# Graph attention and a mixture of experts on one core: one-hots moved from VectorE to ScalarE, segment ends kept on VectorE, weights turned one batch behind the scores

## The chip, the core and the metric

The kernel runs on one core of a Trainium2 chip. PE is TensorE, DVE is VectorE, ACT is ScalarE, POOL is GpSimd and SP is SyncE; SBUF is the working memory and PSUM the memory into which PE writes, here eight banks of 128 partitions x 512 fp32. The metric is the device time of one execution in microseconds (us), the median of three runs.

## The reference, cut to what matters

N = 2500 nodes, E = 80000 edges sorted by destination, H = 4 heads of 64 features.

```python
h = jnp.einsum('nf,hfo->nho', x, W)
e_s = jnp.einsum('nho,ho->nh', h, a_src); e_d = jnp.einsum('nho,ho->nh', h, a_dst)
scores = jax.nn.leaky_relu(e_s[edge_src] + e_d[edge_dst], 0.2)
m = jax.ops.segment_max(scores, edge_dst, num_segments=N)
ex = jnp.exp(scores - m[edge_dst])
denom = jax.ops.segment_sum(ex, edge_dst, num_segments=N)
msg = (ex / denom[edge_dst])[:, :, None] * h[edge_src]
agg = jax.ops.segment_sum(msg, edge_dst, num_segments=N)
x = x + relu(agg)                      # x was normalised before
...
x = x + moe(layernorm(x))              # 8 experts, the best 2 of each node
```

## The kernel before, in words

The execution has three stages. In the first, up to about 110 us, nodes are normalised and projected, a table `h_tab` of 260 fp32 a node (256 features and the 4 source scores) is written to memory, and the layout of the edges in tiles is computed. The third, from about 1142 us on, is the mixture of experts. The change is in the second stage, the edges.

**Edges.** There are 664 tiles (NT) of 128 edges, one edge a partition, laid out so that two neighbouring tiles belong to one block of 128 destination nodes. Eight tiles (BT) are a batch, four batches (PB) or 32 tiles (PH) a round, which the code calls a phase; there are 83 batches (NBAT) and 21 rounds (NPH), the last of 24 tiles.

**Fetches.** POOL fetches tile t with an indirect DMA (L503): for each of the 128 edges the row of `h_tab` of its source goes to slot t % 128 of `ring` in SBUF. It reads the row numbers from `srcP` in SBUF. From tile AHEAD = 80 on it waits, every eight tiles, until batch (t - AHEAD) / 8 is done (`batch_done`).

**Scores and weights of a round.** When all tiles of round f are there, ACT copies their source scores to `Ex` (L839); PE turns these and spreads the destination scores over the partitions (`scores_T`, L606, L610), into bank 6 (`soft`). The layout is now one row for each of 4 heads x 32 tiles. A segment's maximum is found with running maxima: DVE scans each row forwards and backwards (`scores`, L1091 to L1094), PE takes the rows' last columns to one partition (L614, L615), DVE scans along the tiles there (`chain`, L1101 to L1116), PE takes the carries back (`carries_T`, L620), and DVE scans again with them and forms the exponents (`weights`, L1120 to L1132). ACT takes the Exp (L845) and PE turns the weights back (`weights_T`, L631) into bank 5 or 7 (`exT`). If a segment crosses from one round to the next, what its block has collected is rescaled (`rescale`, L1138 to L1142).

**A batch.** DVE multiplies the fetched features in place with the weights and makes the one-hots of the destinations (`weigh`, L1151 to L1153); PE adds, for each pair of tiles, one-hot transposed times features into one of banks 0 to 3 (`batch`, L640); DVE adds the four banks into `acc` (`flush`, L1080). Bank 4 holds the numbers 0 to 127 for the comparison (`iota_ps`). `weigh` of a batch and `flush` of the one before alternate in an order written out by hand; every engine's queue runs in order, so the order of the calls in the loops of DVE, PE and ACT sets the order of the work.

```python
v.tensor_tensor(msg, msg, ex.unsqueeze(3).broadcast_to([P, BT, H, FO]), ALU.mult)
```

is the product of L1151: `msg` is `ring` in SBUF, and `ex` a part of `exT` in PSUM.

## Time and profile before

| | |
|---|---|
| median of 3 runs | 1513.36 us (1510.36 to 1515.03) |
| the profiled execution | 1508.79 us, its span 1507.0 us |
| mean granted clock of PE | 0.755 of full speed |
| busy: PE, DVE, ACT, POOL | 788.1, 757.1, 120.4, 792.2 us |
| fetches of tiles (L503) | 664, from 109.48 to 1067.2 us |
| last addition into `acc` | ends at 1141.8 us |

Busy times are of the whole span. Times in the rows are microseconds from the span's start. A row of the timeline has the start, the duration, the engine, line and operation, what it writes and reads with the shape, how many instructions are merged in the row, and in brackets how long the engine had stood idle before it and what released it. "issue" is time in which the engine waited for nothing that the profile shows, "remote" a release by something the profile can't name. The ends of matmuls are modelled.

### The profile page before, as it was taken

The page shows a single profiled execution, that of the slowest core. Times are in us where ns is not written, and L with a number is a line of the kernel's source. Part 1 is how long each engine was busy: PE and PEld are TensorE (multiplying, and loading weights), DVE is VectorE, ACT ScalarE, POOL GpSimd, SP SyncE. Part 2 cuts the span into 40 slices and gives each one's busy share as a digit, 9 for nine tenths or more (in the row PEclk, how much of TensorE's full clock was granted, in tenths as well). Part 3 has the DMA queues.
Part 4 walks back from the last instruction along what each step waited for, and adds up shares of the span by engine and source line. Part 5 has one row for each costly group of instructions (what it writes and reads, how often), then busy time and mean ns, then how long its engine had stood idle before and what let it go on. Part 6 is the DMA issues. An engine that isn't in the chain of part 4 may idle for free.

```text
span 1507.0 us, 10576 instructions
## 1 busy us (share of the span) xinstructions
PE 788.1 (52%) x2990; PEld 617.4 (41%) x2990; DVE 757.1 (50%) x1578; ACT 120.4 (8%) x289; POOL 792.2 (53%) x843
## 2 busy tenths in 40 slices
PE   0610204454654555644555644545567288888881
PEld 0500203333443343433433433334447266766661
DVE  5510206555576555676555765555878822222215
ACT  3400000000000000000000000000002221111110
POOL 6357763666666666766666766666200034434431
PEclk9865556767787767877768777778776589999985
DMA  8254332333333333333333333333270111111116
GB/s 305 84 74 115 108 85 57 93 91 97 103 95 92 93 97 91 103 94 90 94 97 93 101 94 91 94 98 99 85 265 12 64 44 56 53 52 54 54 48 218
DMA packets 76401, 144.34 MB, mean 96 GB/s; under 512 B 19951, under 2 KB 46749, under 8 KB 76221
## 3 DMA queue, kind: packets, MB, share of 16 engines
q0 software_dynamic: 39856, 110.32, 26.1%
q1 hardware_dynamic: 33909, 30.82, 6.9%
q10 hardware_dynamic: 2584, 2.56, 0.5%
q8 instruction: 25, 0.41, 0.1%
q14 instruction: 27, 0.22, 0.0%
HBM read 126.85 MB, written 17.43 MB: 96 GB/s over the span
## 4 chain that ended last, share of the span: by engine, by line
DVE 33%; another core or an unknown queue 22%; issue 18%; PE 12%; DMA 6%; POOL 5%; DVEq 3%; ACT 2%; SPq 0%; POOLq 0%
DVE acc L1080 8%; DVE shared L1153 6%; DMA ring<-z_tab,ring 4%; DVE ring L1151 4%; PE psum L640 3%; PE psum L736 3%; POOL ys_tab L523 3%; PE psum L750 2%; POOL ring L514 1%; DVEq L1080 1%; PE psum L724 1%; PE psum L569 1%; DVE shared L1387 1%; DVE ring L1152 1%
## 5 line engine op out<-in xcount | busy, mean ns | idle before, releaser
L503 POOL DMA_INDIRECT ring<-h_tab,srcP x664 | 629.1, 947 | 328.9 <-issue 190.1
L640 PE MATMUL psum<-ring,shared 128*128 128x260 f32 x1328 | 417.7, 483 | 236.4 <-DVE acc L1080 156.3
L640 PEld LDWEIGHTS psum<-ring,shared 128*128 128x128 f32 x1328 | 320.2, 247 | 325.1 <-DVE shared L1153 175.2
L1151 DVE TENSOR_TENSOR ring<-ring,psum 128x2048 f32<-128x2048 f32 x83 | 189.5, 2283 | 9.1 <-PE psum L631 2.4
L1080 DVE TENSOR_TENSOR acc<-acc,psum 128x260 f32 x332 | 140.1, 422 | 95.4 <-remote 44.1
L1091 DVE TENSOR_TENSOR_SCAN edY<-RS_all,psum 128x128 f32<-128x128 f32 x21 | 8.8, 421 | 300.8 <-remote 268.5
L523 POOL DMA_INDIRECT ys_tab<-shared,ring x54 | 56.2, 1040 | 150.2 <-DVE shared L1387 142.0
L514 POOL DMA_INDIRECT ring<-z_tab,ring x54 | 52.6, 973 | 151.3 <-DVEq L1367 135.2
L736 PE MATMUL psum<-ring 128*128 128x256 f32 x432 | 114.1, 423 | 29.4 <-DVE ring L1379 29.4
L614 PE MATMUL psum<-ident,Fw 128*1 128x128 f32 x21 | 7.8, 373 | 216.6 <-DVEq L1096 215.0
L1379 DVE TENSOR_SCALAR ring<-psum,tail_consts 128x256 f32<-128x256 f32 x54 | 26.9, 539 | 185.8 <-PE psum L724 182.6
L736 PEld LDWEIGHTS psum<-ring 128*128 128x128 f32 x432 | 89.5, 212 | 49.8 <-DVE ring L1379 36.0
L1153 DVE TENSOR_TENSOR shared<-psum,Dcol 128x1024 f32<-128x1024 f32 x83 | 100.6, 1212 | 0.0
L750 PE MATMUL psum<-ring,RS_all 128*128 x432 | 97.5, 379 | 0.0
L614 PEld LDWEIGHTS psum<-ident,Fw 128*1 128x1 f32 x21 | 1.7, 79 | 225.4 <-DVEq L1096 223.4
L750 PEld LDWEIGHTS psum<-ring,RS_all 128*128 128x128 f32 x432 | 82.1, 190 | 11.2
L888 ACT ACTIVATE RS_all<-psum,tail_consts 128x256 f32<-128x256 f32 x108 | 45.3, 470 | 209.0 <-PE psum L736 191.1
L843 ACT ACTIVATE fm<-old 1x4 f32<-1x4 f32 x20 | 4.1, 204 | 662.0 <-DVE old L1116 534.2
L610 PE MATMUL psum<-X,spread 32*128 32x128 f32 x168 | 43.7, 412 | 0.0
L610 PEld LDWEIGHTS psum<-X,spread 32*128 32x128 f32 x168 | 32.4, 208 | 8.3 <-issue 5.7
L485 POOL DMA_INDIRECT ed_tab<-e_node,spos x20 | 19.6, 982 | 30.6 <-DVE spos L1031 21.9
L724 PE MATMUL psum<-ident,ring 128*128 128x128 f32 x108 | 17.7, 288 | 21.0 <-DMA ring<-z_tab,ring 21.0
(290 smaller groups left out, 656.2 us busy)
## 6 DMA issues: line engine op xcount, KB each, us to landing
ring<-h_tab,srcP POOLq DMA_INDIRECT x664
ring<-in_L_ffn_W SPq DMA_DIRECT2D x16, 512.0 KB, 9.7
h_tab<-ring SPq DMA_DIRECT2D x10, 260.0 KB
ring<-in_x SPq DMA_DIRECT2D x1, 2432.0 KB
z_tab<-ring SPq DMA_DIRECT2D x2, 1024.0 KB, 4.4
ring<-ys_tab SPq DMA_DIRECT2D x4, 512.0 KB, 8.8
ring<-ys_tab ACTq DMA_DIRECT2D x4, 512.0 KB, 9.7
out<-acc SPq DMA_DIRECT2D x4, 512.0 KB
```

Source lines behind the costliest of these rows:

```text
L503: pool.indirect_dma_start(out=ring[:, t % RING, :], out_offset=None, in_=h_tab, in_offset=bass.IndirectOffsetOnAxis(ap=srcP[:, t:t + 1], a ...
L514: pool.indirect_dma_start(out=xs_in[:, u, m, :], out_offset=None, in_=z_tab, in_offset=bass.IndirectOffsetOnAxis(ap=node_ix[:, BM * j + m: ...
L523: pool.indirect_dma_start(out=ys_tab, out_offset=bass.IndirectOffsetOnAxis(ap=dest_ix[:, BM * j + m:BM * j + m + 1], axis=0), in_=y_out[:, ...
L610: last = pe.matmul(soft[:, P:2 * P], spread[:, first:first + P], seeds[:, h, :], start=(h == 0), stop=(h == H - 1))
L640: last = pe.matmul(bank[g][:, 0:MW], dst_oh[:, n % OHB, 2 * g + r, :], ring[:, t % RING, :], start=(r == 0), stop=(r == 1))
L724: last = pe.transpose(bank[u][:, k * BS + m * P:k * BS + (m + 1) * P], xs_in[:, j % XB, m, k * P:(k + 1) * P], ident[:, :])
L736: last = pe.matmul(bank[2 + 2 * u + c // 2][:, c % 2 * BS:(c % 2 + 1) * BS], w1_now[:, u, k, c * P:(c + 1) * P], xsT[:, u, k, :], start=(k ...
L750: last = pe.matmul(bank[6 + u][:, m * F:(m + 1) * F], hT[:, u, c, m * P:(m + 1) * P], w2_all[:, bass.ds(e, 1), c, :].rearrange("p e f -> p ...
L888: act.activation(hT[:, u, c, :], bank[2 + 2 * u + c // 2][:, c % 2 * BS:(c % 2 + 1) * BS], ACT.Gelu, bias=b1_T[:, bass.ds(e * FC + c, 1)]) ...
L1080: v.tensor_tensor(a, a, bank[g][:, 0:MW], ALU.add).then_inc(flushed, 1)
L1151: v.tensor_tensor(msg, msg, ex.unsqueeze(3).broadcast_to([P, BT, H, FO]), ALU.mult)
L1153: v.tensor_tensor(dst_oh[:, n % OHB, :, :], iota_ps.unsqueeze(1).broadcast_to([P, BT, P]), Dcol[:, t0:t0 + BT].unsqueeze(2).broadcast_to([ ...
```

## The change

The one-hots are made on ACT (`one_hots`): the Square of Dcol - iota for each of the eight tiles, and then, for all eight together, the Relu of 1 minus that. There are four buffers of them instead of three. The ends of the segments stay on DVE: the scans write to `runs`, and a transpose in blocks of 32 x 32 (`ends`) puts the end of each row in one line, for each head on a partition of its own; scans over 33 elements and a second such transpose give the carries. For that the tables `links` are copied by SP to the four partitions. The turned weights go to bank 6, and ACT copies them from there to SBUF (`exW`) and makes `fac` (`turned_weights`); `weigh` reads `exW`. The banks freed make seven banks of sums, which the batches take in turn. `weigh` runs two batches ahead of `flush`, and `weights_T` stands behind the batch that follows `scores_T`. AHEAD is 64.

```diff
-    AHEAD = 80
+    AHEAD = 64
...
+        runs = sb("runs", [P, 2, P])
         fac = sb("fac", [P, H])
+        exW = sb("exW", [P, 2, P])
...
-        OHB = 3
-        shared = sb("shared", [P, 3200])
+        OHB = 4
...
-        iota_ps = bank[4][:, 0:P]
+        squared, oh_made = sem("squared"), sem("oh_made")
+        weighed, batch_done, flushed = sem("weighed"), sem("batch_done"), sem("flushed")
         soft = bank[6]
-        exT = (bank[5][:, 0:P], bank[7][:, 0:P])
+        sums = [bank[i] for i in (0, 1, 2, 3, 4, 5, 7)]
+        NSUM = len(sums)
...
+            sp.wait_ge(links_made, 1)
+            for h in range(H):
+                at = h * PH + HEAD_ROW
+                sp.dma_start(links[at:at + 1, :], links[0:1, :]).then_inc(links_in, 16)
...
-                    pe.wait_ge(soft_over, f)
+                    pe.wait_ge(exT_copied, f)
...
-                pe.wait_ge(ends_ready, f + 1)
-                pe.transpose(soft[0:1, 2 * P:3 * P], Fw[:, P - 1:P], ident[:, :])
-                pe.transpose(soft[0:1, 3 * P:4 * P], Bw[:, 0:1], ident[:, :]).then_inc(ends_T, 1)
-
-            def carries_T(f):
-                pe.wait_ge(chain_ready, f + 1)
-                for n, row in enumerate((Cf, Cb)):
-                    last = pe.matmul(soft[:, n:n + 1], row[:, :, :].rearrange("a h t -> a (h t)"),
-                                     ones[0:1, 0:1], start=True, stop=True)
-                last.then_inc(carry_T, 1)
 
             def weights_T(f):
                 if f:
                     pe.wait_ge(oh_row_ready, f)
                     pe.matmul(soft[:, H:2 * H], oh_row[:, :], fm1[:, :], start=True, stop=True)
                 pe.wait_ge(ex_ready, f + 1)
-                if f >= 2:
-                    pe.wait_ge(dst_oh_ready, PB * (f - 1))
-                pe.transpose(exT[f % 2], Ex[:, :], ident[:, :]).then_inc(exT_done, 1)
+                pe.transpose(soft[:, 2 * P:3 * P], Ex[:, :], ident[:, :]).then_inc(exT_done, 1)
...
             def batch(n):
-                pe.wait_ge(dst_oh_ready, n + 1)
+                pe.wait_ge(weighed, n + 1)
+                pe.wait_ge(oh_made, n + 1)
                 for g in range(GB):
-                    if n:
-                        pe.wait_ge(flushed, GB * (n - 1) + g + 1)
+                    G_at = n * GB + g
+                    if G_at >= NSUM:
+                        pe.wait_ge(flushed, G_at - NSUM + 1)
                     for r in range(2):
                         t = n * BT + 2 * g + r
-                        last = pe.matmul(bank[g][:, 0:MW], dst_oh[:, n % OHB, 2 * g + r, :],
+                        last = pe.matmul(sums[G_at % NSUM][:, 0:MW], dst_oh[:, n % OHB, 2 * g + r, :],
                                          ring[:, t % RING, :], start=(r == 0), stop=(r == 1))
                 last.then_inc(batch_done, 1)
...
             for f in range(NPH - 2):
                 n = f * PB
                 batch(n)
                 scores_T(f + 1)
                 batch(n + 1)
-                carries_T(f + 1)
+                weights_T(f + 1)
                 batch(n + 2)
-                weights_T(f + 1)
                 batch(n + 3)
...
+            def one_hots(n):
+
+                if n >= OHB:
+                    act.wait_ge(batch_done, n - OHB + 1)
+                for k in range(BT):
+                    t = n * BT + k
+                    last = act.activation(dst_oh[:, n % OHB, k, :], iota_f[:, :], ACT.Square, scale=-1.0,
+                                          bias=Dcol[:, t:t + 1])
+                last.then_inc(squared, 1)
+                act.wait_ge(squared, n + 1)
+                batch = dst_oh[:, n % OHB, :, :].rearrange("p t d -> p (t d)")
+                act.activation(batch, batch, ACT.Relu, scale=-1.0, bias=ones[:, 0:1]).then_inc(oh_made, 1)
...
+            def turned_weights(f):
+                act.wait_ge(exT_done, f + 1)
+                if f:
+                    act.activation(fac[:, :], soft[:, H:2 * H], ACT.Identity, bias=ones[:, 0:1])
+                if f >= 2:
+                    act.wait_ge(weighed, PB * (f - 1))
+                act.activation(exW[:, f % 2, :], soft[:, 2 * P:3 * P], ACT.Copy).then_inc(exT_copied, 1)
+
+            act.wait_ge(lay_copied, 4)
+            act.wait_ge(links_made, 1)
+            one_hots(0)
+            one_hots(1)
+            scores_of(0)
+            exponents(0)
+            turned_weights(0)
+            for f in range(NPH - 2):
+                n = f * PB
+                one_hots(n + 2)
+                scores_of(f + 1)
+                exponents(f + 1)
+                turned_weights(f + 1)
+                one_hots(n + 3)
+                one_hots(n + 4)
+                one_hots(n + 5)
...
-                    v.tensor_tensor(a, a, bank[g][:, 0:MW], ALU.add).then_inc(flushed, 1)
+                    v.tensor_tensor(a, a, sums[(n * GB + g) % NSUM][:, 0:MW], ALU.add).then_inc(flushed, 1)
...
+            def weights(f):
+
+                rs, rs_back, t0 = RS_all[:, f, 0:P], RS_all[:, f, 1:P + 1][:, ::-1], f * PH
                 v.wait_ge(es_T, f + 1)
                 c.link(v.tensor_tensor_scan(edY[:, :], rs, soft[:, P:2 * P], -BIG, ALU.add, ALU.max))
                 c.link(v.tensor_tensor(S[:, :], soft[:, 0:P], edY[:, :], ALU.add))
-                v.tensor_tensor_scan(Fw[:, :], rs, S[:, :], -BIG, ALU.add, ALU.max)
-                c.link(v.tensor_tensor_scan(Bw[:, ::-1], RS_all[:, f, 1:P + 1][:, ::-1], S[:, ::-1],
+                v.tensor_tensor_scan(runs[:, 0, :], rs, S[:, :], -BIG, ALU.add, ALU.max)
+                c.link(v.tensor_tensor_scan(runs[:, 1, :], rs_back, S[:, ::-1], -BIG, ALU.add, ALU.max))
+
+                c.link(v.transpose(ends[:, 1:1 + 2 * PH], runs[:, :, P - PH:P]))
+                v.tensor_tensor_scan(rowA[:, :], gF[:, f, :], rowF, -BIG, ALU.add, ALU.max)
+                c.link(v.tensor_tensor_scan(rowD[:, ::-1], gB[:, f, :][:, ::-1], rowB[:, ::-1],
                                             -BIG, ALU.add, ALU.max))
-                v.nop().then_inc(ends_ready, 1)
-
-            def chain(f):
-                t0 = f * PH
-                v.wait_ge(ends_T, f + 1)
-                v.tensor_copy(rowF[:, :, 1:PH + 1], soft[0:1, 2 * P:3 * P].rearrange("a (h t) -> a h t", h=H))
-                c.link(v.tensor_copy(rowB[:, :, 1:PH + 1][:, :, ::-1],
-                                     soft[0:1, 3 * P:4 * P].rearrange("a (h t) -> a h t", h=H)))
-                flat = [t[:, :, :].rearrange("a h t -> a (h t)") for t in (rowA, rowF, rowD, rowB)]
-                v.tensor_tensor_scan(flat[0], gw[:, 0, :], flat[1], -BIG, ALU.add, ALU.max)
-                c.link(v.tensor_tensor_scan(flat[2], gw[:, 1, :], flat[3], -BIG, ALU.add, ALU.max))
-                v.tensor_tensor(Cf[:, :, :], rowA[:, :, 0:PH], each_h(cc[:, t0:t0 + PH]), ALU.add)
-                c.link(v.tensor_tensor(Cb[:, :, ::-1], rowD[:, :, 0:PH], each_h(cc[:, t0 + 1:t0 + PH + 1][:, ::-1]),
-                                       ALU.add))
-                v.nop().then_inc(chain_ready, 1)
-                c.link(v.tensor_copy(rowF[:, :, 0], rowA[:, :, PH]))
+                v.tensor_tensor(C[:, 0, :], rowA[:, 0:PH], cc[:, t0:t0 + PH], ALU.add)
+                c.link(v.tensor_tensor(C[:, 1, :], rowD[:, 1:PH + 1], cc[:, t0 + 1:t0 + PH + 1], ALU.add))
+                c.link(v.transpose(carries[:, :, :], C[:, :, :]))
+                c.link(v.tensor_tensor_scan(Fw[:, :], rs, S[:, :], carries[:, 0, PH - 1:PH], ALU.add, ALU.max))
...
-                c.link(v.tensor_scalar(fac[:, :], soft[:, H:2 * H], 1.0, None, ALU.add))
...
                 f, t0 = n // PB, n * BT
                 at, of = t0 % RING, t0 % PH
                 if n % PB == 0:
-                    v.wait_ge(exT_done, f + 1)
-                ex = exT[f % 2].rearrange("p (h t) -> p t h", h=H)[:, of:of + BT, :]
+                    v.wait_ge(exT_copied, f + 1)
+                ex = exW[:, f % 2, :].rearrange("p (h t) -> p t h", h=H)[:, of:of + BT, :]
                 msg = ring[:, at:at + BT, 0:HF].rearrange("p t (h o) -> p t h o", h=H)
                 v.tensor_tensor(msg, msg, ex.unsqueeze(3).broadcast_to([P, BT, H, FO]), ALU.mult)
-                v.tensor_copy(ring[:, at:at + BT, HF:MW], ex)
-                v.tensor_tensor(dst_oh[:, n % OHB, :, :], iota_ps.unsqueeze(1).broadcast_to([P, BT, P]),
-                                Dcol[:, t0:t0 + BT].unsqueeze(2).broadcast_to([P, BT, P]), ALU.is_equal)\
-                 .then_inc(dst_oh_ready, 1)
+                v.tensor_copy(ring[:, at:at + BT, HF:MW], ex).then_inc(weighed, 1)
...
-            scores(0)
-            chain(0)
+            v.wait_ge(links_in, 16 * H)
             weights(0)
-            for f in range(NPH - 2):
+            for f in range(NPH - 1):
                 n = f * PB
                 weigh(n)
-                join(f)
-                scores(f + 1)
+                if f:
+                    flush(n - 2)
                 weigh(n + 1)
+                if f:
+                    flush(n - 1)
+                    rescale(f)
+                weigh(n + 2)
                 flush(n)
-                chain(f + 1)
-                weigh(n + 2)
+                if f < NPH - 2:
+                    weights(f + 1)
+                weigh(n + 3)
                 flush(n + 1)
-                weights(f + 1)
-                weigh(n + 3)
-                flush(n + 2)
-            for f in range(NPH - 2, NPH):
-                first, end = f * PB, min((f + 1) * PB, NBAT)
-                weigh(first)
-                join(f)
-                for n in range(first + 1, end):
-                    weigh(n)
-                    flush(n - 1)
-                if f + 1 < NPH:
-                    scores(f + 1)
-                    chain(f + 1)
-                    weights(f + 1)
+            last = (NPH - 1) * PB
+            flush(last - 2)
+            flush(last - 1)
+            weights(NPH - 1)
+            weigh(last)
+            rescale(NPH - 1)
+            for n in range(last + 1, NBAT):
```

## Rows read from the trace of the kernel before

**Rows 1.** The head of the page.
```profile
span 1507.0 us, 10576 instructions
```

**Rows 2.** Busy time by stage: steady rounds, then the end; us and instructions of each engine.
```profile
279.50:1057.50 778.00, 408.99 (x1394) 308.72 (x1394) 467.71 (x936) 16.09 (x51) 515.46 (x545) 0.75 0.35 95
1057.50:1141.80 84.30, 52.32 (x187) 39.89 (x187) 66.59 (x127) 1.46 (x5) 7.54 (x8) 0.78 0.47 156
```

**Rows 3.** The costliest groups: POOL's fetches of tiles; idle before, by releaser.
```profile
L503 POOL DMA_INDIRECT ring<-h_tab,srcP x664 | 629.1, 947 | 328.9 <-issue 190.1 <-remote 82.4 <-PE psum L640 56.4
```

**Rows 4.** The timeline of one round of 32 tiles, 611 to 646 us.
```profile
611.70 0.95 POOL L503 DMA_INDIRECT ring<-h_tab,srcP  x1 [1.85 <-PE psum L640]
...
620.45 0.95 POOL L503 DMA_INDIRECT ring<-h_tab,srcP  x1 [0.30 <-issue]
...
623.25 0.43 ACT L839 ACTIVATE Ex<-ring 128x128 f32<-128x128 f32 x1 [5.35 <-DMA ring<-h_tab,srcP]
...
629.75 5.43 PE L640 MATMUL psum<-ring,shared 128*128 128x260 f32 x16 [2.35 <-issue]
...
635.22 2.07 PE L610 MATMUL psum<-X,spread 32*128 32x128 f32 x8
...
645.34 0.42 DVE L1091 TENSOR_TENSOR_SCAN edY<-RS_all,psum 128x128 f32<-128x128 f32 x1 [12.04 <-remote]
645.47 0.94 POOL L503 DMA_INDIRECT ring<-h_tab,srcP  x1 [4.07 <-remote]
```

**Rows 5.** Groups of DVE and ACT, each with busy us and mean ns.
```profile
L1151 DVE TENSOR_TENSOR ring<-ring,psum 128x2048 f32<-128x2048 f32 x83 | 189.5, 2283 | 9.1 <-PE psum L631 2.4
L1080 DVE TENSOR_TENSOR acc<-acc,psum 128x260 f32 x332 | 140.1, 422 | 95.4 <-remote 44.1 <-PE psum L640 7.6 <-issue 7.4
L1153 DVE TENSOR_TENSOR shared<-psum,Dcol 128x1024 f32<-128x1024 f32 x83 | 100.6, 1212 | 0.0
...
L1152 DVE COPY ring<-psum 128x32 f32<-128x32 f32 x83 | 15.0, 181 | 0.0
...
L1121 DVE TENSOR_TENSOR_SCAN Fw<-RS_all,carries,S 128x128 f32<-128x128 f32 x21 | 10.2, 484 | 0.8
...
L888 ACT ACTIVATE RS_all<-psum,tail_consts 128x256 f32<-128x256 f32 x108 | 45.3, 470 | 209.0 <-PE psum L736 191.1 <-issue 17.9
...
L845 ACT ACTIVATE Ex<-S 128x128 f32<-128x128 f32 x21 | 6.5, 309 | 162.3 <-DVE S L1127 105.7 <-issue 56.7
...
L845 ACT ACT_TABLE_LOAD x1 | 1.3, 1283 | 0.0
```

**Rows 6.** The timeline of DVE and POOL, 106 to 109 us.
```profile
106.26 0.85 DVE L1059 TENSOR_TENSOR shared<-shared 1x672 f32<-1x672 f32 x1
106.58 1.34 POOL L490 DMA_INDIRECT first_ed<-ed_node,first_i  x1 [0.30 <-issue]
...
108.23 0.94 POOL L490 DMA_INDIRECT first_ed<-ed_node,first_i  x1 [0.31 <-issue]
108.32 0.85 DVE L1065 TENSOR_TENSOR links<-shared,links 1x672 f32<-1x672 f32 x1
```

**Rows 7.** The timeline of the start-up.
```profile
159.73 0.28 DVE L1101 COPY rowF<-psum 1x128 f32<-1x128 f32 x1 [3.94 <-issue]
...
170.31 0.16 DVE L1120 COPY carries<-psum 128x2 f32<-128x2 f32 x1 [8.50 <-remote]
...
216.91 0.94 POOL L503 DMA_INDIRECT ring<-h_tab,srcP  x1 [7.59 <-remote]
...
245.56 0.94 POOL L503 DMA_INDIRECT ring<-h_tab,srcP  x1 [18.96 <-PE psum L640]
```

**Rows 8.** The timeline of the end: the last fetch and the last flush.
```profile
1066.20 0.97 POOL L503 DMA_INDIRECT ring<-h_tab,srcP  x1 [0.30 <-issue]
...
1139.66 2.13 DVE L1080 TENSOR_TENSOR acc<-acc,psum 128x260 f32 x4 [2.34 <-PE psum L640]
```

120 lines of the change are left out of this document (56 added, 64 removed).

## Prediction, made before the changed kernel was run

> **What bounds the kernel now.** The page comes first: one core, a span of 1507.0 us, and in it no engine busy for more than about half of the time [rows 1]. So I ask where the work stands still, stage by stage. The stage that the change touches, from the first fetch of an edge tile to the last addition into `acc`, runs from 109.5 to 1141.8 us, and its steady part is 279.5 to 1057.5: there DVE is busy 60%, PE 53%, POOL 66%, ACT 2% [rows 2]. That part handles 544 of the 664 tiles, 17 rounds of 32 tiles, in 778 us: 45.8 us a round.
>
> The view of POOL's line says what it does in the rest. 664 indirect fetches at 947 ns [rows 3], each with 0.30 us behind it that no wait explains, come every 1.25 us: 40.0 us for a round's 32. The remainder is waiting, 82.4 + 56.4 us over the whole stream [rows 3]. In the timeline of one round [rows 4] the two gaps are seen: 1.85 us before 611.70 and 4.07 us before 645.47. So a round is 40.0 us of fetching plus 5.8 us of waiting, and POOL is the bound wherever it does not wait.
>
> What ends the 4.07 us is the odd thing. PE's `batch` for tile group n runs by its rows from 629.75 to 635.2 and the score matmuls of L610 from 635.22 to 637.3, but DVE, which waits for those (L1091), starts at 645.34, 8 us after they ended, and POOL, which waits for `batch_done`, starts at 645.47, 10 us after [rows 4]. Both waits are put down to "remote", that is to nothing the profile can name. Both end together, and always about 4 us after POOL has stopped. I take it as a fact of this trace: after some 20 us of unbroken fetching PE's increments arrive late, and a stop of POOL lets them through.
>
> **What the change takes away.** On DVE: the one-hot of L1153, 1.21 us x 83 = 100.6 us [rows 5]. The walk through PE for the segment ends (two transposes, then carries back) becomes two 32 x 32 transposes on DVE; the three operations on one partition that copied and four-fold spread (L1088, L1101, L1102) go. A round's DVE work was 0.60 x 45.8 = 27.5 us [rows 2]; with 1.5 us as an estimate for the latter (five operations of 0.3), it becomes 27.5 - 4 x 1.21 - 1.5 = 21 us. None of this is on the bound: POOL's 40.0 us lie beside it. By itself it is worth nothing in a round.
>
> **What it adds on ACT.** Per batch eight Squares of 128x128 and one Relu of 128x1024. Nearest rows: 0.31 us for an Exp of 128x128, 0.47 us for 128x256 with a bias per partition [rows 5]. Eight at 0.31 and one Relu at 0.31 + 896 columns x (0.47 - 0.31)/128 = 1.4 us (an upper value, the 0.47 has a bias the 0.31 has not) make 3.9 us; bounds 3.3 and 4.5. Four a round: 16 us on an engine that is 2% busy. Hidden, as long as the order of ACT's queue doesn't bite: the one-hots of the last batch of a round stand behind `turned_weights`, which waits for DVE, PE and the fetches. Both engines' chain from "last tile of the next round fetched" to "last batch of this round done" is: landing and copy of the scores 3.2 us (620.45 the fetch of that tile, 623.25 + 0.43 the copy) [rows 4], L610 and its transpose 2.5 (2.07 the first [rows 4]), `weights` on DVE 5.5 (six scans at 0.4 to 0.5 as L1121 [rows 5], ten short ones), Exp, turn and copy 1.2, one-hots 3.9, the batch 5.4 [rows 4]: 21.7 us, plus the 10 us of fetches before. The limit of 64 tiles asks for this within 40. It holds with 8 us to spare, if increments come on time. One link is tighter: the second batch of a round now stands behind the score matmuls, ends 3.2 + 2.5 + 5.4 = 11.1 us after the last fetch, and is wanted at 10.0. That costs 1 us a round even with nothing late.
>
> **What it costs on POOL.** This is the term that decides. Before, `weigh` (L1151) had one operand in SBUF (`ring`) and one in PSUM (`exT`). Now both are in SBUF (`ring`, `exW`). What a DVE operation with two SBUF operands does to a fetch is shown in [rows 6]: L1059 ran from 106.26 to 107.11, the fetch of 106.58 began inside it and took 1.34 us instead of 0.94. It ended 0.40 late, which is what of L1059 was left, 0.53, less 0.13. The fetch of 108.23 began 0.09 us before a like operation (L1065) and lost nothing. So a fetch that begins while such an operation runs waits for its end; one that begins first does not. `weigh` takes 2.28 us [rows 5], longer than POOL's beat of 1.25, so every one catches a fetch: the next begins on average 0.62 us into it and waits 2.28 - 0.62 - 0.13 = 1.5 us. Some 77 of the 83 come while fetches are still going: 77 x 1.5 = 116 us, plus about 5 for the copy behind each and the extra short pairs: 121 us, or 6.2 us a round. Bounds: 0, if the long form with a broadcast operand does not do what L1059 did; 77 x 2.15 = 166.
>
> The Trainium skill ("SBUF — State Buffer", Who interferes with whom) bears on this: a VectorE instruction with two SBUF inputs excludes a GpSimd instruction that reads SBUF, and the one that starts first keeps the ports to its end; the first half of the trace's pattern agrees, with 0.40 us. The same section infers that `tensor_tensor` does not hold up descriptor generation; by that the term would be 0, and it is the third rival.
>
> **The sum.** Last fetch: 109.5 + 663 x 1.25 = 938 without any wait; it was 1066.2 [rows 8], so waits were 128. New: 121 for the ports. Start-up: the two waits of 7.59 and 18.96 us [rows 7] were 26. The first weights come some 12 us earlier, since the idle of 8.50 before L1120 [rows 7] and another of about 4 go, but the stream stops at tile 64 instead of 80; I take 20 (10 to 26). Steady: a round's late increments. With 64 tiles, POOL wants a round's first batch 18 us after PE has finished it. In the round shown it had not come 8 us after PE's end (637.3 to 645.3) and came with the stop of POOL; in the start-up too POOL went on only 7.59 us after it had stopped [rows 7]. Fetching is now less often interrupted, and PE's work in a round is less only by the two end transposes and the two carries, so I expect one stop a round as now, 4.07 - 0.30 = 3.8 us, 18 times: 68 us. Bounds 1.0 (above) and 6. Together 938 + 121 + 20 + 68 = 1147, 81 later than before.
>
> The tail gets it partly back. From last fetch to last flush it was 1139.66 + 2.13 - 1066.20 = 75.6 us [rows 8], for ten batches that DVE was behind with. With at most eight groups ahead and a slower stream, about six are left: landing, scores, `weights` and turn 3.2 + 2.5 + 5.5 + 1.2 = 12.4, three times weigh 2.5 and flush 2.1 ([rows 5, 8]), rescale 1 and a last batch 5.4 make 20.2, and 5 for the batch or two that stand before the scores on PE: 38 us (29 to 45), 38 less. What follows 1141.8 is untouched.
>
> 81 - 38 = +43. The profiled execution took 1508.8 us (its span and 1.8 around it), 0.3% under the median of 1513.4 of the three runs shown, so one and the other are one figure here. 1508.8 + 43 = **1552 us**.
>
> **Rivals.**
> 1. *Ports block, but increments come on time.* For it: PE's late increments fall where DVE is idle (637 to 645) and never where DVE is busy (the batch that ended POOL's wait at 611.70 was on time [rows 4]); in the new order DVE works nearly through all of PE's batches, and each blocked fetch is itself a small stop. Against: the stops that let increments through were 4 us long. Steady waits become 18 x 1 = 18 instead of 68: 1552 - 50 = 1502. With a few less or more us of port waiting this lies between 1480 and 1520, on either side of no change. It decides where the steady wait falls under 1.4 us a round.
> 2. *The ports don't block* (the reading of the inference above, as a mechanism: the fetch needs only a short look at its indices, which slips in). POOL's 121 goes; the tail is then longer, 45 to 55, for compute is again behind. 1552 - 121 + 12 = 1443 with late increments, less without. For it: several short two-operand operations passed unseen; against: all of these ended less than 0.13 us into the fetch or began after it. This one ends on the other side: faster.
> 3. *ACT's queue is the bound.* One late `gap_made` or `z_ready` holds one-hots for three batches, and with a late increment (10 us) the chain of 31.7 reaches 42, over 40; with 46 for the ports it just fits. If the late increments hit the links twice a round, 4 us more each: 18 x 4 = 72, 1624.
> 4. *A table load on ACT* at every change between Exp and Square would be 2 x 1.3 us a round [rows 5], inside the slack; its chance is part of rival 3's.
>
> **Chances.** Forecast (ports block, one stop a round) 0.47, own range 1525 to 1590; rival 1 0.30, of which 0.19 under -0.3%, 0.07 within, 0.04 over; rival 2 0.15; rival 3 0.08. Runs of this kernel lie within 0.3%, so that is what a measurement can tell from no change. Faster 0.35, same 0.07, slower 0.58. The range takes in rival 2's end and leaves rival 3 and the fastest part of rival 2: 1440 to 1590.
>
> **What would show it.** Right: fetches with durations of 1.5 to 3 us, one beside each `weigh`, POOL's mean for L503 at 1.10 to 1.15 us instead of 0.95; a round near 50 us with one wait of about 4 put down to "remote"; DVE busy under half of a round. Rival 1: the long fetches, but rounds of 47. Rival 2: all fetches at 0.95. Rival 3: PE waiting for `oh_made`. The prediction is wrong if DVE gets the shorter end (`weigh` waits for fetches and grows), or if late increments have to do with how much PE does at a stretch rather than with POOL's going on.

## The result, and the profile after

The changed kernel takes 1526.15 us (median of 4, 1523.85 to 1529.0) beside 1513.28 for the kernel before (4 runs): ratio 1.0088, 95% interval 1.0064 to 1.0112. It is slower by 13 us. The direction was forecast, and the time lies in the range; but the forecast was 43 us slower, over three times too much (and 1552 us in all, 26 more than measured, since it was added to a profiled execution that lay 4.5 us under the median).

Every set of runs below has its own runs of the kernel before. In five sets these took 1506 to 1514 us, in two 1355 and 1356; a kernel is compared only inside its set, and where a set is of the second kind I say so.

The page after, its head and the groups that answer to [rows 1, 3, 5]:

```profile
span 1523.3 us, 10850 instructions
...
L511 POOL DMA_INDIRECT ring<-h_tab,srcP x664 | 736.7, 1109 | 281.2 <-issue 196.1
...
L830 ACT ACTIVATE shared<-iota_f,Dcol 128x128 f32<-128x128 f32 x664 | 201.9, 388 | 17.2 <-DVE links L1110 17.2
...
L1173 DVE TENSOR_TENSOR ring<-ring,exW 128x2048 f32<-128x2048 f32 x83 | 190.2, 2292 | 4.7 <-ACT exW L860 1.5
L1119 DVE TENSOR_TENSOR acc<-acc,psum 128x260 f32 x332 | 140.5, 423 | 85.7 <-remote 31.4
...
L835 ACT ACTIVATE shared<-shared,ones 128x1024 f32<-128x1024 f32 x83 | 95.3, 1149 | 2.7
```

The first group holds the price. POOL was busy 629.1 us with its 664 fetches and idle 328.9 before them [rows 3]; now it is 736.7 and 281.2: 107.6 more in the fetches themselves, 47.7 less in waits. With a first fetch 2.2 us later that puts the last one 62 us later (1128.3 beside 1066.2). The other part of the result lies behind it: from there to the last flush it is 34.5 us instead of 75.6, and what follows is 4.8 us shorter, which leaves 16 us between the two spans. DVE's product takes what it took (2292 ns beside 2283).

Busy time in the steady stretch of [rows 2]:

```profile
279.50:1057.50 778.00, 332.11 (x1186) 265.58 (x1187) 335.39 (x751) 234.81 (x631) 561.21 (x507) 0.67 0.33 88
```

DVE is down from 60% to 43% (335.4 of 778), ACT up from 2% to 30%, and POOL, the bound, up from 66% to 72%. In this stretch the relief of DVE brought nothing; the load on POOL is the price.

The timeline of DVE and POOL beside three products, 705 to 717 us:

```profile
705.24 2.29 DVE L1173 TENSOR_TENSOR ring<-ring,exW 128x2048 f32<-128x2048 f32 x1
706.70 1.64 POOL L511 DMA_INDIRECT ring<-h_tab,srcP  x1 [4.16 <-remote]
...
708.65 0.95 POOL L511 DMA_INDIRECT ring<-h_tab,srcP  x1 [0.30 <-issue]
709.69 2.29 DVE L1173 TENSOR_TENSOR ring<-ring,exW 128x2048 f32<-128x2048 f32 x1
709.90 2.90 POOL L511 DMA_INDIRECT ring<-h_tab,srcP  x1 [0.30 <-issue]
...
713.11 0.94 POOL L511 DMA_INDIRECT ring<-h_tab,srcP  x1 [0.31 <-issue]
714.35 2.33 DVE L1173 TENSOR_TENSOR ring<-ring,exW 128x2048 f32<-128x2048 f32 x1
714.35 0.95 POOL L511 DMA_INDIRECT ring<-h_tab,srcP  x1 [0.30 <-issue]
715.60 1.89 POOL L511 DMA_INDIRECT ring<-h_tab,srcP  x1 [0.30 <-issue]
```

This is the pattern of [rows 6] at full size. The fetch of 709.90 begins 0.21 us into the product, which ends at 711.98, and takes 2.90 instead of 0.95 us: it ends 0.82 us after the product (0.95 - 0.13). The fetch of 714.35 begins with the product and is untouched; the next one, which begins 1.25 us into it, takes 1.89.

The timeline of the one stop of a round, 743 to 756 us, which answers to [rows 4]:

```profile
743.55 0.43 ACT L843 ACTIVATE Ex<-ring 128x128 f32<-128x128 f32 x1 [21.78 <-DMA ring<-h_tab,srcP]
...
746.53 5.82 PE L638 MATMUL psum<-ring,shared 128*128 128x260 f32 x16
...
746.71 0.42 DVE L1126 TENSOR_TENSOR_SCAN edY<-RS_all,psum 128x128 f32<-128x128 f32 x1 [22.44 <-PE psum L618]
...
750.77 0.95 POOL L511 DMA_INDIRECT ring<-h_tab,srcP  x1 [0.30 <-issue]
...
751.61 0.14 DVE L1151 COPY ends<-rowA 128x1 f32<-128x1 f32 x1
...
754.12 0.29 DVE L1153 TENSOR_SCALAR oh_row<-iota_f,links 128x128 f32<-128x128 f32 x1 [2.37 <-remote]
...
755.93 1.64 POOL L511 DMA_INDIRECT ring<-h_tab,srcP  x1 [4.21 <-remote]
```

An increment is the step by which an engine raises a semaphore that another waits for. PE's batch ends by its rows at 752.35; the trace records its increment of `batch_done` at 755.67, and POOL, which has stood since 751.72, goes on at 755.93. In the same 4 us even DVE's increment to itself (L1151 to L1153) takes 2.37 us. The stop comes before tiles 104, 136, 168 and so on, each of which waits for the second batch of a round, the one behind the score matmuls.

The start-up, which answers to [rows 7], and the last flush, to [rows 8]:

```profile
201.08 0.94 POOL L511 DMA_INDIRECT ring<-h_tab,srcP  x1 [5.92 <-remote]
...
214.00 0.95 POOL L511 DMA_INDIRECT ring<-h_tab,srcP  x1 [3.11 <-remote]
...
1128.30 0.95 POOL L511 DMA_INDIRECT ring<-h_tab,srcP  x1 [0.30 <-issue]
...
1160.72 2.13 DVE L1119 TENSOR_TENSOR acc<-acc,psum 128x260 f32 x4 [1.94 <-PE psum L638]
```

### The profile page after: what moved, and what is told of

It reads as the page before. It is cut to its first block, busy times and chain, and to the rows that moved or that the text cites. A ratio compares the mean times of both kernels' runs of the same rounds, so it can differ in the third digit from the quotient of the medians.

```text
span 1523.3 us, 10850 instructions
## 1 busy us (share of the span) xinstructions
PE 723.6 (48%) x2864; PEld 586.9 (39%) x2864; DVE 636.1 (42%) x1432; ACT 418.2 (27%) x1076; POOL 898.9 (59%) x843
## 4 chain that ended last, share of the span: by engine, by line
POOL 53%; issue 17%; PE 7%; another core or an unknown queue 7%; DMA 6%; DVE 6%; ACT 2%; DVEq 1%; SPq 0%; POOLq 0%
POOL ring L511 48%; DMA ring<-z_tab,ring 4%; POOL ys_tab L531 3%; PE psum L730 2%; POOL ring L522 1%; PE psum L718 1%; DVE shared L1395 1%; PE psum L744 1%; PE psum L638 1%; ACT ring L766 1%; DVEq L1391 1%; PE psum L685 1%; DVE acc L1436 1%; PE psum L577 1%
## 5 line engine op out<-in xcount | busy, mean ns | idle before, releaser
L511 POOL DMA_INDIRECT ring<-h_tab,srcP x664 | 736.7, 1109 | 281.2 <-issue 196.1
L638 PE MATMUL psum<-ring,shared 128*128 128x260 f32 x1328 | 376.3, 451 | 11.5 <-DVE ring L1174 7.1
L638 PEld LDWEIGHTS psum<-ring,shared 128*128 128x128 f32 x1328 | 301.8, 231 | 78.7 <-issue 10.3
L614 PE MATMUL psum<-ident,Ex 128*128 128x128 f32 x21 | 10.0, 474 | 511.7 <-ACT Ex L843 412.0
L830 ACT ACTIVATE shared<-iota_f,Dcol 128x128 f32<-128x128 f32 x664 | 201.9, 388 | 17.2 <-DVE links L1110 17.2
L1173 DVE TENSOR_TENSOR ring<-ring,exW 128x2048 f32<-128x2048 f32 x83 | 190.2, 2292 | 4.7 <-ACT exW L860 1.5
L843 ACT ACTIVATE Ex<-ring 128x128 f32<-128x128 f32 x21 | 9.0, 427 | 467.0 <-DMA ring<-h_tab,srcP 467.0
L730 PE MATMUL psum<-ring 128*128 128x256 f32 x432 | 106.6, 403 | 29.4 <-DVE ring L1387 29.4
L730 PEld LDWEIGHTS psum<-ring 128*128 128x128 f32 x432 | 84.1, 200 | 47.7 <-DVE ring L1387 36.0
L835 ACT ACTIVATE shared<-shared,ones 128x1024 f32<-128x1024 f32 x83 | 95.3, 1149 | 2.7
L625 PE MATMUL psum<-fm,oh_row 128*128 128x4 f32 x40 | 9.9, 319 | 66.2 <-DVE fm L1155 45.6
```

Of the source, the lines that this page charges most:

```text
L511: pool.indirect_dma_start(out=ring[:, t % RING, :], out_offset=None, in_=h_tab, in_offset=bass.IndirectOffsetOnAxis(ap=srcP[:, t:t + 1], a ...
L638: last = pe.matmul(sums[G_at % NSUM][:, 0:MW], dst_oh[:, n % OHB, 2 * g + r, :], ring[:, t % RING, :], start=(r == 0), stop=(r == 1))
L730: last = pe.matmul(bank[2 + 2 * u + c // 2][:, c % 2 * BS:(c % 2 + 1) * BS], w1_now[:, u, k, c * P:(c + 1) * P], xsT[:, u, k, :], start=(k ...
L830: last = act.activation(dst_oh[:, n % OHB, k, :], iota_f[:, :], ACT.Square, scale=-1.0, bias=Dcol[:, t:t + 1])
L835: act.activation(batch, batch, ACT.Relu, scale=-1.0, bias=ones[:, 0:1]).then_inc(oh_made, 1)
```

## The experiments

"Ports" is the time by which fetches were longer than 0.946 us, "start" and "steady" the waits of POOL before tile 100 and from there on, above the 0.30 us behind every fetch, "end" the time from the last fetch to the last flush. All rows are of the profiled execution; in e2 and e3 that one took 7 and 8 us more than the median, and their executions spread over 21 and 19 us.

| | before | changed | e1 | e2 | e3 | e4 | e11 |
|---|---|---|---|---|---|---|---|
| ports | 1 | 108 | 4 | 119 | 117 | 3 | 113 |
| start | 26 | 8 | 14 | 24 | 19 | 24 | 6 |
| steady | 101 | 71 | 95 | 10 | 34 | 99 | 69 |
| last fetch | 1066 | 1128 | 1054 | 1092 | 1111 | 1063 | 1126 |
| end | 76 | 35 | 43 | 70 | 45 | 68 | 35 |
| span | 1507 | 1523 | 1458 | 1525 | 1517 | 1494 | 1522 |

**e1: weights in PSUM again.**

```diff
-        exW = sb("exW", [P, 2, P])
-        sums = [bank[i] for i in (0, 1, 2, 3, 4, 5, 7)]
+        sums = [bank[i] for i in (0, 1, 2, 3, 4)]
+        exP = (bank[5][:, 0:P], bank[7][:, 0:P])
...
-                act.activation(exW[:, f % 2, :], soft[:, 2 * P:3 * P], ACT.Copy).then_inc(exT_copied, 1)
+                act.activation(exP[f % 2], soft[:, 2 * P:3 * P], ACT.Copy).then_inc(exT_copied, 1)
```

> The changed kernel with the turned weights copied by ACT into PSUM (banks 5 and 7, a round each) instead of into SBUF, so that the product of L1173 has one operand in SBUF and one in PSUM as in the kernel before; for that five banks of sums are left instead of seven. Theory 1 (a fetch that begins while a product with two SBUF operands runs waits for its end): the 75 fetches over 1 us go, the mean of L511 falls from 1.11 to 0.95 us, and the 108 us by which the fetches were long go from POOL's line; the one stop of 4.2 us a round stays, a round is 44 us instead of 49.2, the last fetch starts near 1020 us, the end behind it grows from 36 to about 45 us, the span is 1424 us. Rival (the compute is close behind, and a faster POOL only waits longer): the fetches are short too, but the stops grow by 2 to 5 us a round, 1460 to 1510. Rival (the long fetches have to do with something else in the new order, such as ACT's reading of SBUF): nothing changes, 1523.

1458.76 us beside 1506.22: ratio 0.968 (0.9651 to 0.9707), faster than both kernels. The fetches' group, and two stops of the timeline:

```profile
L511 POOL DMA_INDIRECT ring<-h_tab,srcP x664 | 632.5, 953 | 311.4 <-issue 192.0 <-remote 115.8 <-PE psum L638 3.6
```

```profile
600.22 0.95 POOL L511 DMA_INDIRECT ring<-h_tab,srcP  x1 [3.11 <-remote]
...
657.16 0.94 POOL L511 DMA_INDIRECT ring<-h_tab,srcP  x1 [4.37 <-remote]
```

The long fetches are gone, and with e11 below (banks alone) and e2 (the same cost put into the kernel before) that makes the second operand in SBUF their cause. But 30 of the 104 us came back as waits (281.2 to 311.4): 31 steady waits instead of 18. So the fetches did what both theory and rival said; the waits grew as the rival said, but by 1.4 us a round instead of 2 to 5, and the span of 1458 lies between the theory's 1424 and the rival's 1460 to 1510.

**e11: five banks with the weights in SBUF** (the first diff's line of banks alone).

> The changed kernel with five banks of sums instead of seven, weights in SBUF as in it: the part of the first experiment that came along with moving the weights. Theory 1 (all that the first experiment won came from the ports): the same as the changed kernel, 1520 to 1530, ports 108, one stop of 4.2 us a round. Rival (fewer banks hold PE back so that batches come later, or spread the products over the round): another pattern of stops, 10 to 40 us either way.

1522.83 us beside 1505.73, 1.0110 (1.0092 to 1.0128), ports 113: the banks play no part in what e1 won.

**e2: the kernel before with the weights in SBUF.** ACT copies `exT` to `exW` behind `exT_done`, and `weigh` waits for that and reads it:

```diff
-                ex = exT[f % 2].rearrange("p (h t) -> p t h", h=H)[:, of:of + BT, :]
+                ex = exW[:, f % 2, :].rearrange("p (h t) -> p t h", h=H)[:, of:of + BT, :]
```

> The kernel before with one thing added: ACT copies the turned weights from PSUM to SBUF, and the product reads them there (two SBUF operands). Theory 1: one long fetch for each of some 77 products, mean of the fetches 1.10 us, about 105 us more on POOL's line. Of a round's two waits the one of 1.8 to 2.8 us, which ends with PE's batch, is mostly swallowed (POOL asks later), so 3 us more a round, 60 us, and the last fetch near 1126; the end behind it gets shorter by 10 to 25 us: 1540 to 1560 in all from 1508.8. Rival (compute sets the pace and takes the delays in): at most 15 us more.

1520.55 us beside 1506.22: 1.0072 (1.0042 to 1.0102). My 1540 to 1560 was missed; the rival's "at most 15 us more" fits the medians.

```profile
L505 POOL DMA_INDIRECT ring<-h_tab,srcP x664 | 746.8, 1125 | 236.8 <-issue 199.1 <-PE psum L642 19.9 <-remote 17.9
```

117.7 us more in the fetches, and 92.1 less in waits (328.9 to 236.8). In the old order the products come 6 to 26 us apart (in the changed kernel about 5, and once a round 35), so the long fetches break the stream more often: the longest unbroken stretch in the steady part is 20 fetches, before it was 24. Of 35 steady waits 4 are left. That each long fetch serves as a small pause is my first rival's mechanism, and it fits; but the increments are not on time for it. By the trace's record of `batch_done`, 24 of 73 come over 1 us after the batch's end (before: 34 of 72). A slower POOL also asks for them later, and e2 does not tell the two apart.

**e4: one-hots on ACT alone**, in the kernel before (`one_hots` as in the change, four buffers).

> The kernel before with the one-hots on ACT and nothing else of the change (four buffers of them; ends of the segments through PE, weights in PSUM, four banks of sums, 80 tiles ahead as before). By the prediction's step DVE's 1.21 us a batch are worth nothing on POOL's line, where the fetches set 40 of 45.8 us: last fetch at 1066, the end behind it shorter by 8 to 10 batches of 1.2 us where DVE is behind: 1497 to 1509. Rival (the second wait of a round, 1.8 to 2.8 us, ends with a batch that DVE's one-hot held up): up to 2 us x 20 less as well, 1460 to 1475. Rival (ACT's queue holds the one-hots up behind the exponents): slower, 1520 or more.

1498.52 beside 1506.22, 0.9966 (0.9932 to 1.0), at best a small gain: last fetch 3 us earlier, end 8 us shorter, as expected. The waits moved from 24 + 8 fetches apart (4.1 + 2.2 us) to 16 apart (3.0 each), and their sum stayed.

**e3: the second batch ahead of the score matmuls**, in the changed kernel.

```diff
-                scores_T(f + 1)
                 batch(n + 1)
-                weights_T(f + 1)
+                scores_T(f + 1)
                 batch(n + 2)
+                weights_T(f + 1)
                 batch(n + 3)
```

> The changed kernel with PE's queue in another order: the second batch of a round stands ahead of the score matmuls (batch n, batch n+1, scores, batch n+2, turned weights, batch n+3) instead of behind them. The one stop of POOL in a round (4.2 us) ends with that second batch. Theory 2 (PE's increments arrive late once POOL has been fetching for some 20 us, and a stop lets them through): the second batch is now announced early, but the third takes its place, one stop of about 4 us a round stays, 1519 to 1523 us. Rival (the stop is this batch's place in the queue: it starts only when the scores are through): the stops go, a round is 45.2 us, 18 x 4 = 72 us less on POOL's line, and the end behind it grows by some 10: 1460 us.

1510.27 beside 1506.22, 1.0026 (1.0 to 1.0051). Between the two, theory (1519 to 1523) and rival (1460): another batch ends the stops, but they are 1.3 to 3.4 us instead of 4.2, and a long fetch lies 6 tiles ahead of them instead of 23. At the start the third batch, now behind the scores, costs 13.9 us.

**e8: e1 and e3 together.**

> The first and the third experiment together: turned weights in PSUM, and the second batch of a round ahead of the score matmuls. Theory 3: other batches end the stops, their sum a round stays 5.5 to 6 us, 1455 to 1465. Rival (places in the queue): half the stops go, 43 us a round, 1410 to 1430.

1487.88 beside 1512.11 (0.9839, 0.9806 to 0.9873): 49 steady waits, together 112 us. Theory and rival (1455 to 1465, 1410 to 1430) are both missed. Without port pauses the better place in PE's queue is worth nothing here, a loss against e1 (0.968).

**e7: 128 tiles ahead, on e1.**

> The first experiment's kernel with up to 128 tiles ahead instead of 64. Theory 3 in its simplest form (a fixed need of 1.43 us a fetch): rounds of 46 us, only the start-up gets shorter by 14 us and the end part longer by as much, 1450 to 1465. Variant (a long unbroken stretch is paid with a stop that grows less than in proportion, as 5.9 us after 64 and 7.6 after 80 fetches at the start): fewer and longer stops, a fetch at 1.35 to 1.40, rounds of 43.5 to 45, 25 to 40 us less on POOL's line, end part 15 to 20 longer, 1430 to 1450. Rival (the stops are waits for batches late by their place in the queue, which 64 more tiles cover): no stops, rounds of 40.2, compute sets the end: 1400.

1514.94 beside 1512.11, 1.0011 (0.9992 to 1.003): all three forecasts (1400 to 1465) are missed. The steady waits stay (110 us, 30 of them, one of 22 before tile 144) and a round stays at 46, as the simplest form says. But the end grows from 43 to 102 us, since compute may be 16 batches behind at the last fetch; that I had put at 15 to 20.

**e6 and e10: half the matmuls; half the bytes**, on e1.

```diff
-                    for r in range(2):
-                        t = n * BT + 2 * g + r
+                    t = n * BT + 2 * g
...
-                                         ring[:, t % RING, :], start=(r == 0), stop=(r == 1))
+                                     ring[:, t % RING, :], start=True, stop=True)
```

is e6; in e10, from tile 128 on:

```diff
-                    out=ring[:, t % RING, :], out_offset=None, in_=h_tab,
+                    out=ring[:, t % RING, MW // 2:MW], out_offset=None,
+                    in_=h_tab.rearrange("n (x f) -> (n x) f", x=2),
```

> The first experiment's kernel with only the first tile of each pair multiplied and added by PE (the other half of the messages is left out of the sums), so PE's work in a batch is halved. Theory 3 (the late increments go with POOL's unbroken fetching): stops of 3.0 us after 16 and 4.3 after 24 fetches as before, rounds of 46 us, at most 10 us less in the end part. Rival (they go with the amount of PE's work since the last stop, or PE is simply slower than its rows show): stops half as long or gone, rounds of 42 to 43, 60 us less.

> The first experiment's kernel with rows of half the length fetched from tile 128 on (130 fp32 instead of 260, to the second half of the slot; the first half keeps old features, and the table is read as twice as many rows, so the sums are of other numbers): as many fetches and descriptors, half the bytes. Theory 3a (what needs 1.43 us a fetch is the moving of the bytes, which POOL's issuing at 1.25 us runs ahead of): the stops go, a round is 40.2 us plus true waits of 1 to 2, 80 us less in the span. Theory 3b (it is the issuing itself, by fetch and not by byte): stops of 3.0 us after 16 and 4.3 after 24 fetches stay, 1455 to 1460.

Both leave out part of the work, and their sums are other numbers. Each ran once, in another set than e1. Spans 1454.6 and 1458.1 beside e1's 1457.8; the steady waits 93 and 96 us beside 95. Neither half of PE's matmuls nor half of the bytes changes the sum of the waits, though in e6 they lie otherwise. Two of the ten stops after 32 unbroken fetches that e6 shows:

```profile
838.49 0.95 POOL L511 DMA_INDIRECT ring<-h_tab,srcP  x1 [5.44 <-remote]
883.95 0.95 POOL L511 DMA_INDIRECT ring<-h_tab,srcP  x1 [5.45 <-remote]
```

In most of these runs a stop (the idle time in front of a fetch, its usual 0.30 included) goes by the unbroken fetches ahead of it:

| fetches at 1.25 us without a pause | stop, us, mean (how many, where) |
|---|---|
| 16 | 3.0 (18 in e1, 28 in e4, 17 in e10) |
| 24 | 4.1 (18 before), 4.3 (11 in e1), 4.4 (12 in e10) |
| 21 to 24, then a stop, in the changed kernel | 4.0 to 4.5 (18) |
| 32 | 5.4 (10 in e6) |

Some do not fit: those after 24 in e6 run from 0.7 to 4.7 us (8), e4 has one of 7.6 after 24, e8 one of 9.3 after 16, and stops after 8 are anything from 0.5 to 5.1 us.

**e5, e9: pauses put in by hand**, on e1: one, then three small memsets on POOL behind every fetch, each waiting for the one before.

```diff
+                for k in range(3):
+                    if t or k:
+                        pool.wait_ge(rested, 3 * t + k)
+                    pool.memset(rest[:, :], 0.0).then_inc(rested, 1)
```

> The first experiment's kernel (turned weights in PSUM) with a small memset on POOL behind every fetch, which waits for the memset before it; 0.1 to 0.25 us each, 3 to 8 us a round. In the runs so far a stop of POOL is 3.0 us after 16 unbroken fetches, 4.1 to 4.3 after 24, wherever the batch stands that it waits for, and with stops and port waits together a fetch has cost 1.43 to 1.46 us in all but the changed kernel. Theory 3 (pauses of POOL are needed in proportion to its fetches, and it doesn't matter how they are spread): the small rests take the place of the stops, a round stays at 46 us, 1455 to 1475. Rival (each stop is a wait for a batch that is really late by its place in the queues): the rests come on top as far as the batches don't catch up, up to 52 us a round, 1500 to 1580.

> The first experiment's kernel with three small memsets on POOL behind every fetch, each waiting for the one before, instead of the one of the fifth experiment (which at 0.12 us fitted into the 0.30 us that lie behind a fetch anyway and left its beat at 1.25 us, so that it tested nothing). Three should bring the beat to 1.45 to 1.55 us, 46.5 to 49.5 us a round without any stop. Theory 3 (fetches and increments together need about 1.43 us a fetch, and it doesn't matter how the pauses are spread): the stops go or shrink to under 1 us, a round is 32 beats, the span 1457.8 plus 20 x (32 beats - 46). Rival (a stop of 3 to 4 us comes after every 16 to 24 fetches whatever their beat): 6 us a round on top of the beats, a span of 1560 or more.

e5, 1472.66 beside 1512.11 (0.9731), left the beat at 1.25 us and so tested nothing: stops as in e1. e9, run once, has a beat of 1.54 us and a span of 1545.0:

```profile
L512 POOL DMA_INDIRECT ring<-h_tab,srcP x664 | 632.1, 952 | 112.6 <-issue 23.6
L519 POOL MEMSET rest<- 128x8 f32 x1992 | 216.7, 109 | 77.1
```

"remote" is gone from the line. Every round is 49.8 us, 32 x 1.54 and 0.6 more, the longest distance between two fetches is 2.15 us, and all 78 recorded increments of `batch_done` lie within 0.03 us of the end of their batch (in e1: 22 of 70). The longer beat also leaves the work more time, so e9 alone does not show that the stops were no true waits for work; e17 below does.

**e12 to e16: two memsets** (a beat of 1.38 us). e12 (on e1), e13 (before), e14 (changed) and e15 (e1 with e3) fell into a set of the second kind, the kernel before at 1354.96; e16 repeats e12 in one of the first.

> The first experiment's kernel (weights in PSUM) with two small chained memsets on POOL behind every fetch. In the ninth experiment three of them made the beat 1.54 us, and no stop was left in any round, nor at the start; a round was 32 beats. Two should make it 1.39 us. Theory 3 (about 1.43 us a fetch are needed, pauses may lie anywhere): short stops of 1 to 2 us a round in all, rounds of 45 to 46, the 14 us of stops at the start gone: 1435 to 1450 against 1458.8. Rival (there is a rate between 1.25 and 1.54 below which stops come in full): stops of 3 to 4 us after every 16 to 24 fetches on top, rounds of 50, 1530.

> The kernel before with the same two memsets behind every fetch. Theory 3: its stops of 4.1 us after 24 fetches go or shrink to 1 us, those of 1.8 to 2.8 us after 8 are partly true waits and may stay; rounds of 45 to 46.5 instead of 45.8, the two waits at the start (26 us) shrink by 8 or more: 1485 to 1505. Rival (the stops there wait for batches that are late by their place in the queues): 4.5 us more a round, 1590.

> The changed kernel (weights in SBUF) with the same two memsets. Theory 3: the stop of 4.2 us a round goes, since the 23 fetches ahead of it are no longer unbroken at 1.25 us; the long fetches stay (108 us); a round is 32 x 1.39 + 5.4 = 49.9 against 49.3, the start 8 us shorter: 1518 to 1530, no change. Rival (the memsets meet the ports too, and wait as the fetches do, but then the products catch fewer fetches): 10 us either way. Rival (the stop is a true wait): 1600.

> The twelfth experiment's kernel once more. It ran on a chip on which the kernel before took 1355 us, while on the four chips of the other runs (the first profile among them) it took 1506 to 1513; no stop was seen there, but none may have been there without the memsets either. On a chip of the 1510 kind: theory 3 says a beat of 1.39 us, stops of 1 to 2 us a round in all, rounds of 45 to 46, 1435 to 1455, faster than the first experiment's 1459; the rival says stops of 3 to 4 us on top, 1500 to 1530. On a chip of the 1355 kind it repeats 1429.

e12 1429.30, e13 1451.28, e14 1540.39, e15 1434.69: all slower than 1354.96, which tells of the memsets (664 times 0.13 us, some 90), not of stops, and e14 carries the ports besides. e14 against e13 is the change at equal beat: 89 us, with ports of 120. e15 is 5 us behind e12, as expected, so the place in PE's queue gains nothing there. e16 took 1477.03 beside 1514.39 (0.9746), a smaller gain than e1's in its set (0.968): one stop of 1.9 us a round above the beat is left, rounds of 46.6, so the beat of 1.38 shrinks the stops but costs more than it saves. My 1435 to 1455 was missed. This expectation lays the kinds to the chip; but the record has the same chip number for both sets, so that is not borne out.

**e17, e18: e1 and the changed kernel again.** This set was of the second kind too, the kernel before at 1356.23.

> The first experiment's kernel once more (weights in PSUM, five banks of sums), to see it beside the kernel before in another set of runs. In a set in which the kernel before takes 1506 to 1514 us: 1459 again, stops of 3.0 and 4.3 us. In a set in which it takes 1355: if the 150 us are the stops and late increments, there are none here either, the stream is bound by POOL's beat in both, last fetch near 935, and the two kernels are within 15 us of each other.

> The changed kernel once more, unaltered, for the same reason. Beside a kernel before of 1506 to 1514 us: 1526 again, 0.5 to 1.2% slower. Beside one of 1355: the ports still cost their 108 us or more and nothing is given back for them, since there are no stops to take the place of: about 110 on POOL's line, less 35 in the end part, 1425 to 1445, 5 to 6.5% slower.

e17 took 1342.89, 0.9902 (0.9886 to 0.9919), within the 15 us expected; e18 1476.23, **1.0888** (1.087 to 1.0906), well above my 1425 to 1445. The fetches' line in e17 and then in e18, by duration and by what ended the idle time:

```profile
L511 POOL DMA_INDIRECT ring<-h_tab,srcP x664: 940/946/1077, 96.2 to 941.6; - x166
...
  issue: 195.3, 641
  PE psum L638: 23.0, 23
```

```profile
L511 POOL DMA_INDIRECT ring<-h_tab,srcP x664: 945/949/3083, 97.1 to 1077.4; - x166
...
  issue: 197.0, 646
  PE psum L638: 15.7, 18
```

No "remote" in either, and every recorded increment of `batch_done` (83 and 82) lies within 0.03 us of the end of its batch. e17 is e1's kernel at e1's beat of 1.25 us, and its stops of 3 to 4 us are gone: these were no waits for work. It needs 40.9 us a round, with one true wait of 0.9 us on average above the 0.30: PE's batch ends at 635.88 and POOL goes on at 636.15.

```profile
636.15 0.94 POOL L511 DMA_INDIRECT ring<-h_tab,srcP  x1 [1.30 <-PE psum L638]
```

In e18 the ports cost 141 us, and the steady waits are 9 us instead of 16: next to nothing is left to give back. Its span of 1473.1 is 133.8 over e17's 1339.3, and 120 us over the kernel before by the medians.

## Why the prediction was wrong in size

| step | forecast | measured |
|---|---|---|
| ports | 121 | 108, 75 long fetches at 1.45 us (I had 77 at 1.5, and 5) |
| start-up waits | 20 (10 to 26) | 8.4, and the first fetch 2.2 later |
| steady stops | 18 x 3.8 = 68 | 18, together 70.6 |
| last fetch | 1147 | 1128.3 |
| end | 38 (29 to 45) | 34.5 |
| what follows the last flush | as before, 365.2 | 360.4 |
| against the span before | +43 | +16.3 |
| medians | the same | +12.9 |

- **Mechanism: right.** Fetches that begin inside a product wait for its end; the mean of L511 is 1.109 us (said: 1.10 to 1.15), rounds average 49.4 (said: near 50), one wait of 4.2 put down to "remote", DVE under half. e1, e2 and e11 isolate it. The Trainium skill ("SBUF — State Buffer", Who interferes with whom) infers that `tensor_tensor` does not hold up descriptor generation; the fetch of 2.90 us, and the 4 us of ports with one operand in PSUM, speak against that for a product of 2.3 us with two SBUF operands. That inference stands behind rival 2 of the list, which the prediction once calls the third.
- **The terms that failed** are the start-up (20, measured 8.4) and the ports (121, measured 108); with the first fetch, the end, the last stage and the steady stops (12.5 + 11.6 - 2.2 + 3.5 + 4.8 - 2.6) and 3.4 between spans and medians they make the 30 us, but for a rounding of 1. Of the ports' 12.5, 7.5 are fewer and shorter hold-ups (75 x 1.45, not 77 x 1.5) and 5 the copies and short pairs, which hardly show. The start-up lay even below my lower bound. I moved only the first weights; but the wait of 18.96 [rows 7] was for a batch that stood in PE's queue behind `scores_T`, which then itself waited for DVE's ends. That wait inside `scores_T` is gone from the change. The kernels that keep it (e2, e4) have 18.9 and 16.5 us there, those without it (changed, e1) 3.1 and 3.8. It is not isolated: before, PE then stood another 3.45 us for a flush, and e3, which has lost the wait but puts the third batch behind the scores, has 13.9.
- **Steady stops: right in size, wrong in place.** I expected the round's first batch to end the stop; it is the second, which by my sum is 1 us late when increments come on time. e17 shows that wait alone, 0.9 us. The 3.8 us were carried over from the stop before, though another batch ends it now, so the good fit is in part luck.
- **Rival 1** (a blocked fetch is itself a small stop, so increments come on time) comes out in e2 by its time, 118 us paid, 92 returned, though many increments stay late there. In the changed kernel the four products follow each other right behind the stop, then 23 fetches run unbroken, and the stop is that of 23 fetches. So its pauses fall where they are not needed. Rivals 2 and 3 are refuted: long fetches exist, ACT's 3.6 us a batch (2.43 + 1.15) are hidden, for no wait of PE is put down to the one-hots. Of rival 4, ACT in the changed kernel loads no table between 155 and 1177 us.
- **Whose 13 us?** In the first kind of set the kernel before carries 127 us of such waits, and the change takes 48 of them back. Where they are absent it costs 120, and the verdict is 9% instead of 0.9%. Of the 107 us between the two costs, 48 are these waits and 32 the longer port time of e18; the rest can't be placed, as no trace shows the kernel before in a set of the second kind.

**Left open:** what delays the increments, and what makes a set of runs free of it. By what was tried, not the amount of PE's work (e6) or of the bytes (e10), and not a batch's place (e4, e8).

## What to carry to other kernels

Where POOL issues indirect fetches without a break, keep one operand of a long DVE product in PSUM: here, moving it to SBUF cost one hold-up for nearly each product of 2.29 us (75 for 83), 1.45 us on average. e1, the change with that one operand put back, beats the kernel before in both kinds of sets (0.968 and 0.990). Relieving DVE, busy 60%, by its one-hots was worth 0.3% (e4), since POOL sets the beat; look for what a move does to the engine that does. And before a wait is priced as work that is late, compare it with the end of that work by its own rows.

## What the runs showed of the hardware

In five sets increments arrive late during unbroken fetching at 1.25 us: of those of `batch_done` that the traces record, 34 of 72 come over 1 us after the batch's end in the kernel before, 43 of 70 in e1, 20 of 74 in the changed kernel. A stop that ends the lateness is mostly 3.0 us after 16 fetches, 4.3 after 24, 5.4 after 32, that is 1.41 to 1.42 us a fetch with its share of the stop (32 x 1.25 + 5.4 - 0.3 is 45.1 for 32); at 1.54 us there are none, at 1.38 one of 1.9 a round. During the stop DVE's own increments are late too (2.37 us). In two of seven sets none of this is seen, and every kernel is 48 to 158 us quicker; about 14 us of that lie ahead of the first fetch of a tile (96.2 in e17, 110.7 in e1). One trace of the changed kernel from either kind, by the view of its fetches: the second prints a row that the first lacks,

```profile
DMA to landing us min/median/max: 2.7/2.8/5.7
```

because it holds 10622 of the 10624 landing increments (664 x 16); the first holds 5663, the kernel before 3131, e9 8314. The traces of the kernel before, the changed one and e18 would have late increments and lost records go together, but e9 has all increments on time with 2310 landings lost, and e2 holds little more than the kernel before (3692). That the recording of events delays the increments is a guess that no run tests.
